# Folding the softmax normalisation into the attention loop and coarsening the interleaved weight quantisation, on eight cores

## The chip, the cores and the metric

The kernel runs on the 8 cores of one Trainium2 chip, each core with half of one sequence of four. The metric is the device time in microseconds of the slowest core. There is no traffic between the cores; each works out keys and values for its whole sequence of 4096 tokens and everything else for its own 2048 tokens.

## The reference

The reference is one transformer layer: multi-head attention with low-rank projections and a rotary part, then a feed-forward block whose weights are quantised to three levels and whose activations are quantised to 8 bits.

```python
attn = softmax(einsum('bhqd,bhkd->bhqk', query, key) / scale)     # 16 heads of 64
out = einsum('bhqk,bhkd->bhqd', attn, value)
x = x + layernorm(out @ Wo + bo)
m = mean(abs(w)); wq = clip(round(w / m), -1, 1) * m              # w_gate, w_up, w_down
x = x + layernorm(bitlinear(silu(bitlinear(h, gate)) * bitlinear(h, up), down))
```

The division by the sum of the softmax can be made after the product with the values. That division, and the quantisation of the three weights, are what the change is about.

## The kernel before

Every operation is put into a list for its engine, and a helper writes out each list in order; an engine takes its instructions strictly in that order and waits on semaphores. All compute carries line 335 in the profile and all transfers line 56, since helpers record them, so groups are told apart by tiles: `poolF` is the f32 buffer on chip, `poolB` the bf16 one, `p` are the PSUM banks and `pb` the PSUM bank for bf16 transposes.

The stages follow one another: projections (to line 768), attention, a normalisation pass (lines 1075 to 1107), the output projection with layer norm, and the feed-forward block.

**Attention** (`emit_b_pair`, line 914) runs over 8 pairs of heads. A pair loads its queries, keys and values, and these loads wait for the pair's predecessor to have spilled its result. Then it runs over 4 query tiles of 512; below, one such tile of one pair is a *slot*, so there are 32 slots, numbered 0 to 31. In a slot 32 chunks of 128 keys are worked through: `emit_scores` (three bf16 matmuls per head), the exponential on ScalarE, and `emit_av` (one f32 matmul per head, with a column of ones in the values, so that row 64 of the result is the sum of the exponentials). The scores of a chunk stand ahead of the product of the chunk before it. After the last chunk comes `drive()`, one step of the weight quantisation, and then for each head three VectorE instructions that empty the PSUM bank: the upper bf16 half, the remainder, and the row of sums, which a transfer takes to the buffer `dall`. The first `emit_av` of the next slot waits for these, its scores do not. At the end of the pair two transfers on POOL's queue spill the unnormalised result.

**Weight quantisation** (`make_wquant`, line 809) is cut into 39 steps, of which 32 are driven by the slots and the last 7 follow after the attention. Each of the weights has mean steps (loads and absolute sums on VectorE), a chain (the mean by way of two tiny matmuls, with bank `p[6]`), and quantisation steps: for each tile a load, three VectorE instructions, then for every 8 blocks of 128 columns 8 transposes on TensorE into `pb`, one VectorE copy, and 8 transfers on POOL's queue. The next 8 transposes wait for the 8 transfers to have landed. A tile of `wg` and `wu` has 8 such blocks (one round), a tile of `wd` has 32 (four rounds). The slots go: 0 to 3 means of `wg`, 4 its chain, 5 to 12 its quantisation at 4 tiles a slot, 13 to 16 means of `wu`, 17 chain, 18 to 25 quantisation, 26 to 29 means of `wd`, 30 chain, 31 the first tile of `wd`. Seven tiles of `wd` follow behind the last pair.

**The normalisation pass** waits for the weight `wo`, takes the reciprocal of all sums at once (16 partitions by 2048), and then for each pair loads the two halves from memory, and for each of four query tiles broadcasts the reciprocals over the partitions with a matmul into `p[6]`, adds the halves, multiplies, splits again, and at the end spills. The next pair's loads wait for that spill.

Of the kernel before, what the change touches and what calls it, by code (L numbers as in the profile page):

```python
# [9 lines left out]
ALU = mybir.AluOpType  # L10
# [9 lines left out]
T_OWN = 2048  # L20
NH = 16
# [165 lines left out]
def build_nc():  # L187
# [47 lines left out]
    attnU_hi_s = scr("attnU_hi", (D, T_OWN), BF16)  # L235
    attnU_lo_s = scr("attnU_lo", (D, T_OWN), BF16)
# [31 lines left out]
    sg_all = af.alloc(16)  # L268
    su_all = af.alloc(16)
    sd_all = af.alloc(16)  # L270
    dall = af.alloc(2048)
    PERSIST_F = af.mark()

    identb = ab.alloc(128)
# [2 lines left out]
    P = Prog(nc)  # L277
# [19 lines left out]
    for j, (src_off, dst) in enumerate(((0, bvb_bc), (1024, bwo_bc))):  # L297
        for half in range(2):
# [3 lines left out]
                start=True, stop=True))(),  # L302
                after=[ev_b1, ev_b2, ev_c[6]] + bc_ev[-1:])
# [14 lines left out]
                   after=[ev_s1])  # L318
# [3 lines left out]
        after=[ev_s2, ev_s3])  # L322
# [466 lines left out]
    ab.reset(PERSIST_B)  # L789
    v_sb = af.alloc(4160)  # L790
    aT = [af.alloc(512), af.alloc(512), af.alloc(512), af.alloc(512)]
    dstage = af.alloc(1024)

    qh_sb = ab.alloc(2048); ql_sb = ab.alloc(2048)
    kh_sb = ab.alloc(4096); kl_sb = ab.alloc(4096)
# [1 line left out]

    wtile0 = af.alloc(4096)
    qa = af.alloc(4096)
    qb = af.alloc(4096)  # L800
    wtile = [wtile0, qa]
    rcols = af.alloc(32)
    wt_b = ab.alloc(4096)
# [1 line left out]

    wq_steps = []
    wq_last = [e_mcols]

    def make_wquant(wdram, ntiles, ncols, nblk, wT_scr, m_col, thr_col):
        st_ = {"prev": [None], "prev_l": [None, None], "prev_tr": [None],  # L810
# [18 lines left out]
        def chain():  # L829
            def go():  # L830
                red_evs = st_["red"]
                e_acc = E("vector", red_evs, "reduce_sum", cols[:, 28:29],
                          rcols[:, 0:ntiles], axis=AX.X)
                e_ps = E("tensor", [e_acc], "matmul", p[6][0:1, 0:1],
                         cols[:, 28:29], onecol_c[:, 0:1], start=True, stop=True)
# [9 lines left out]
                e_thr = E("scalar", [e_bc], "activation", out=thr_col[:, 0:1],  # L845
                          in_=p[6][:, 4:5], func=ACT.Copy, scale=0.5)
                st_["prev_l"] = [list(wq_last) + [e_m, e_thr]]
                st_["prev_tr"] = [list(wq_last) + [e_m, e_thr]]
                wq_last[:] = wq_last[:] + [e_thr]
            return go  # L850
# [46 lines left out]
    wg_m, wg_c, wg_q, wg_st = make_wquant(wg, 32, D, 8, wgT_s, mgate_c, cols[:, 32:33])  # L897
    wu_m, wu_c, wu_q, wu_st = make_wquant(wu, 32, D, 8, wuT_s, mup_c, cols[:, 33:34])
    wd_m, wd_c, wd_q, wd_st = make_wquant(wd, 8, INNER, 32, wdT_s, mdown_c, cols[:, 34:35])
    wq_steps = (  # L900
        [wg_m(8 * i, 8 * i + 8, [e_mcols]) for i in range(4)] + [wg_c()] +
        [wg_q(4 * i, 4 * i + 4) for i in range(8)] +
        [wu_m(8 * i, 8 * i + 8, [e_mcols]) for i in range(4)] + [wu_c()] +
        [wu_q(4 * i, 4 * i + 4) for i in range(8)] +
        [wd_m(2 * i, 2 * i + 2, [e_mcols]) for i in range(4)] + [wd_c()] +
        [wd_q(i, i + 1) for i in range(8)]
    )

    b_prev_loads = [e_mcols]
    b_prev_spills = list(a2b_done[-1:])  # L910
    attn_spills = []
    wq_slices = []

    def emit_b_pair(pr, start_evs, drive=None):
        loads = []
# [18 lines left out]
        em2 = E("vector", [loads[-1]], "memset", vv[:, :, 129:130], 1.0)  # L934
        ev_ld = loads + [em1, em2]

        dstage_free = {0: list(start_evs), 1: list(start_evs)}
        d_dmas = []
        exp_done = {}
        av_done = {}  # L940
        evac_done = [None, None]
        for qt in range(4):
            def emit_scores(chn):
                par = chn % 2
# [40 lines left out]
                    av_done[(hd_, par)] = e_av  # L985

            emit_scores(0)
            emit_scores(1)
            for chn in range(2, 32):
                emit_av(chn - 2)  # L990
                emit_scores(chn)
            emit_av(30)
            emit_av(31)
            if drive is not None:
                drive()
            for hd_ in range(2):
                e_u = E("vector", [av_done[(hd_, 0)], av_done[(hd_, 1)]],
                        "tensor_copy",
                        au_hi[64 * hd_:64 * hd_ + 64, 512 * qt:512 * qt + 512],
                        p[4 + hd_][0:64, 0:512])  # L1000
                e_u2 = E("vector", [e_u], "tensor_tensor",
                         au_lo[64 * hd_:64 * hd_ + 64, 512 * qt:512 * qt + 512],
                         p[4 + hd_][0:64, 0:512],
                         au_hi[64 * hd_:64 * hd_ + 64, 512 * qt:512 * qt + 512],
                         ALU.subtract)
                slot = (2 * qt + hd_) % 2
                e_d = E("vector", [e_u2] + dstage_free[slot], "tensor_copy",
                        dstage[0:1, 512 * slot:512 * slot + 512],
                        p[4 + hd_][64:65, 0:512])
                e_dd = P.dma("gpsimd",  # L1010
                             dall[2 * pr + hd_:2 * pr + hd_ + 1,
                                  512 * qt:512 * qt + 512],
                             dstage[0:1, 512 * slot:512 * slot + 512],
                             after=[e_d], lane=f"b_d{slot}")
                dstage_free[slot] = [e_dd]
                evac_done[hd_] = e_d
                d_dmas.append(e_dd)
        s1 = P.dma("gpsimd", attnU_hi_s[128 * pr:128 * pr + 128, :],
                   au_hi[:, 0:T_OWN], after=[evac_done[0], evac_done[1]],
                   lane="b_au")  # L1020
        s2 = P.dma("gpsimd", attnU_lo_s[128 * pr:128 * pr + 128, :],
                   au_lo[:, 0:T_OWN], after=[evac_done[0], evac_done[1]],
                   lane="b_au")
        return [s1, s2] + d_dmas[-2:] + [evac_done[0], evac_done[1]]

    pair_done = b_prev_loads
    wq_i = [0]
# [5 lines left out]

    for pr in range(8):
        pair_done = emit_b_pair(pr, pair_done, drive=wq_drive)
        attn_spills += pair_done[:4]
    while wq_i[0] < len(wq_steps):
        wq_steps[wq_i[0]]()
        wq_i[0] += 1
# [7 lines left out]
    ab.reset(PERSIST_B)  # L1047
    xqT_sb = ab.alloc(16384)
    PERSIST_B2 = ab.mark()
    dinv = af.alloc(2048)  # L1050
    dexp = af.alloc(512)
    anf = af.alloc(1024)
    projb2 = [af.alloc(1024), af.alloc(1024)]
    xrow2 = [af.alloc(1024), af.alloc(1024)]
    x2row2 = [af.alloc(1024), af.alloc(1024)]
# [16 lines left out]
    ev_wo = prep_w_hilo(wo, (4, 4), 128, wstage3,  # L1072
                        wo_hi[:, 4096:8192], wo_lo[:, 4096:8192], [ev_wo])

    e_dinv = E("vector", attn_spills + [ev_wo], "reciprocal",
               dinv[0:NH, 0:T_OWN], dall[0:NH, 0:T_OWN])

    cn_done = []
    prev_cn = [e_dinv]
    prev_p6 = [e_dinv]  # L1080
    for pr in range(8):
        lh = P.dma("sync", au_h[:, 0:T_OWN],
                   attnU_hi_s[128 * pr:128 * pr + 128, :], after=prev_cn)
        ll = P.dma("sync", au_l[:, 0:T_OWN],
                   attnU_lo_s[128 * pr:128 * pr + 128, :], after=prev_cn)
        sp_evs = []
        for qt in range(4):
            e_bc2 = E("tensor", [e_dinv] + prev_p6, "matmul", p[6][:, 0:512],
                      sel_sb[0:NH, 128 * pr:128 * pr + 128],
                      dinv[0:NH, 512 * qt:512 * qt + 512], start=True, stop=True)  # L1090
            sl = slice(512 * qt, 512 * qt + 512)
            e_t = E("vector", [e_bc2, lh, ll], "tensor_tensor", anf[:, 0:512],
                    au_h[:, sl], au_l[:, sl], ALU.add)
            e_n = E("vector", [e_t], "tensor_tensor", anf[:, 512:1024],
                    anf[:, 0:512], p[6][:, 0:512], ALU.mult)
            e_h2 = E("vector", [e_n], "tensor_copy", au_h[:, sl],
                     anf[:, 512:1024])
            e_l2 = E("vector", [e_h2], "tensor_tensor", au_l[:, sl],
                     anf[:, 512:1024], au_h[:, sl], ALU.subtract)
            prev_p6 = [e_n]  # L1100
            sp_evs.append(e_l2)
        s1 = P.dma("gpsimd", attnU_hi_s[128 * pr:128 * pr + 128, :],
                   au_h[:, 0:T_OWN], after=sp_evs, lane="cn_sp")
        s2 = P.dma("gpsimd", attnU_lo_s[128 * pr:128 * pr + 128, :],
                   au_l[:, 0:T_OWN], after=sp_evs, lane="cn_sp")
        prev_cn = [s1, s2, sp_evs[-1]]
        cn_done = [s1, s2, sp_evs[-1]]

    def ln_single(src, after, b=36):
        e_s = E("vector", after, "reduce_sum", stats[:, b:b + 1], src, axis=AX.X)  # L1110
# [473 lines left out]
```

How the kernel before makes its waits and increments, by code:

```python
        def run(eng_obj, e):  # L115
# [7 lines left out]
                        if val == 0:  # L123
                            continue
                    elif a.dma and a.lane is None:
                        sem, val = a.sem, max(a.val, q_total_at(a.eng, ev.seq))
                    else:
                        sem, val = a.sem, a.val
                    key = id(sem)
                    if key not in waits or waits[key][1] < val:
                        waits[key] = (sem, val)
                for sem, val in waits.values():
                    eng_obj.wait_ge(sem, val)
                ins = fn(eng_obj)
                if ev.needed and ins is not None:
                    ins.then_inc(ev.sem, 16 if ev.dma else 1)
```

## Time and profile before

| what | us |
|---|---|
| median of 2 runs (10101.92 and 10256.78) | 10179.35 |
| the profiled execution's own time | 9708.83 |
| its span, slowest core (5) | 9707.3 |
| shortest span of a core (0) | 9655.7 |
| PE busy in that span | 6200.5 (64%) |
| DVE busy | 2211.1 (23%) |
| ACT busy | 2218.5 (23%) |
| POOL busy | 885.3 (9%) |

In the profile PE is TensorE's matmuls, PEld its weight loads, DVE VectorE, ACT ScalarE, POOL GpSimd, SP SyncE; PEclk is the granted TensorE clock as a share of full speed. The chain of work that ended last is 58% PE, 15% DVE and 9% DMA. The mean of a busy share says little here, because the stages have different limits: attention is read slot by slot.

### The profile page before, as it was taken

The numbers are of one execution on the slowest core, as the hardware profiler recorded it, in microseconds if no ns is written. First come the engines' busy times: TensorE is split into PE (matmuls) and PEld (weight loads), VectorE is DVE, ScalarE is ACT, GpSimd is POOL, SyncE is SP. The second block draws the span as 40 slices with busy tenths as digits, with TensorE's granted clock in tenths as the row PEclk, the third lists the DMA queues.
The fourth block names the chain that finished last, engine by engine and source line by source line (L and its number), as shares of the span: only waits on it lengthen the run. The fifth ranks groups of instructions, "written<-read, shape, count | busy, mean of one in ns | idle before, by whom it ended". The sixth has DMA issues, their size and how long they took to land.

```text
span 9707.3 us, 78875 instructions; the slowest of 8 cores (9655.7 to 9707.3 us)
## 1 busy us (share of the span) xinstructions
PE 6200.5 (64%) x21142; PEld 1966.1 (20%) x21142; DVE 2211.1 (23%) x2749; ACT 2218.5 (23%) x3070; POOL 885.3 (9%) x1453
## 2 busy tenths in 40 slices
PE   5765556776877667578776766687831255454439
PEld 2332222231211111112111111121210022121214
DVE  3323222221101110111001010111012465534442
ACT  1112111113433223234332322233310011111101
POOL 0100212120000110100001010100023010000000
PEclk8776778888998889799997988899965578677769
DMA  4881222212110010211101001002011223343334
GB/s 88 95 86 52 77 78 74 78 61 70 31 26 18 21 45 14 50 33 31 44 11 46 14 27 39 21 36 61 9 45 55 83 78 117 97 138 113 122 105 139
DMA packets 386848, 588.61 MB, mean 61 GB/s; under 512 B 127195, under 2 KB 287084, under 8 KB 378262
## 3 DMA queue, kind: packets, MB, share of 16 engines
q1 hardware_dynamic: 329366, 436.56, 15.7%
q0 software_dynamic: 57088, 147.00, 7.2%
q8 instruction: 223, 3.65, 0.2%
q14 instruction: 171, 1.40, 0.1%
HBM read 436.52 MB, written 146.80 MB: 60 GB/s over the span
## 4 chain that ended last, share of the span: by engine, by line
PE 58%; DVE 15%; issue 10%; DMA 9%; POOL 4%; ACT 2%; SPq 1%; DVEq 0%; POOLq 0%; ACTq 0%; PEldq 0%
PE p L335 55%; DVE poolF L335 10%; DVE poolB L335 4%; PE pb L335 3%; POOL poolF L335 2%; ACT poolF L335 2%; DMA poolF<-vp 1%; POOL wdT L56 1%; DMA poolF<-lo_sk 1%; SPq L56 1%; POOL wuT L56 1%; POOL wgT L56 1%; DMA wuT<-poolB 1%; DMA wgT<-poolB 1%; DMA poolF<-wd 1%
## 5 line engine op out<-in xcount | busy, mean ns | idle before, releaser
L335 PE MATMUL p<-poolB 128*128 128x512 bf16 (+1 forms) x14976 | 3466.9, 397 | 1052.8 <-DVE poolF L335 783.6
L335 PE MATMUL p<-poolF 128*65 128x512 f32 (+3 forms) x4750 | 2486.7, 611 | 1329.6 <-PE p L335 524.6
L335 ACT ACTIVATE poolF<-p,poolF 128x512 f32<-128x512 f32 x2576 | 1962.3, 762 | 5522.7 <-PE p L335 5354.0
L335 PEld LDWEIGHTS p<-poolB 128*128 128x128 bf16 (+1 forms) x14976 | 1321.9, 99 | 3692.3 <-issue 2759.5
L335 PEld LDWEIGHTS p<-poolF 128*65 128x65 f32 (+3 forms) x4750 | 500.3, 143 | 2735.6 <-issue 2733.2
L335 PE MATMUL pb<-poolB 128*128 128x128 bf16 x1408 | 311.3, 257 | 1095.4 <-DVE poolB L335 460.6
L335 DVE TENSOR_TENSOR poolF<-poolF 128x512 f32<-128x512 f32 (+3 forms) x689 | 452.3, 658 | 1353.0 <-ACT poolF L335 1028.5
L335 DVE COPY poolB<-pb 128x1024 bf16<-128x1024 bf16 (+1 forms) x288 | 128.8, 480 | 2724.1 <-PE pb L335 2722.8
L335 DVE TENSOR_SCALAR poolF<-poolF 128x1024 f32<-128x1024 f32 (+4 forms) x529 | 437.6, 827 | 226.0 <-DMA poolF<-wd 102.4
L335 ACT ACTIVATE poolF<-poolF 128x1024 f32<-128x1024 f32 (+2 forms) x194 | 121.6, 627 | 1404.8 <-DVE poolF L335 1129.9
L335 DVE TENSOR_REDUCE poolF<-poolF 128x1 f32<-128x1024 f32 (+3 forms) x205 | 322.7, 1574 | 349.8 <-ACT poolF L335 168.3
L335 PEld LDWEIGHTS pb<-poolB 128*128 128x128 bf16 x1408 | 142.1, 103 | 1279.1 <-issue 1179.8
L335 DVE CAST poolB<-p 64x512 bf16<-64x512 f32 x64 | 43.7, 683 | 1248.1 <-PE p L335 1240.7
L335 POOL TENSOR_TENSOR poolF<-poolF 128x512 f32<-128x512 f32 (+1 forms) x240 | 252.0, 1050 | 815.6 <-ACT poolF L335 780.4
L56 POOL DMA_DIRECT2D wgT<-poolB x256 | 144.6, 573 | 1205.7 <-DVE poolB L335 1195.3
L56 POOL DMA_DIRECT2D wuT<-poolB x256 | 143.4, 568 | 1209.8 <-DVE poolB L335 1197.7
L56 POOL DMA_DIRECT2D poolF<-poolF x64 | 31.8, 497 | 1615.3 <-DVE poolF L335 1610.7
L56 POOL DMA_DIRECT2D wdT<-poolB x256 | 135.8, 538 | 401.7 <-DVE poolB L335 390.1
L335 DVE CAST poolB<-poolF 128x512 bf16<-128x512 f32 (+1 forms) x102 | 84.6, 830 | 362.6 <-ACT poolF L335 250.0
L335 DVE TENSOR_TENSOR poolB<-poolF,poolB 128x512 bf16<-128x512 f32 (+1 forms) x102 | 152.8, 1498 | 11.3 <-DVE poolB L335 0.9
L335 POOL TENSOR_SCALAR poolF<-poolF 128x1 f32<-128x1 f32 (+1 forms) x196 | 40.4, 206 | 1216.6 <-DVE poolF L335 1200.5
L335 ACT ACTIVATE poolF<-poolB 128x512 f32<-128x512 bf16 x96 | 60.7, 632 | 313.1 <-DVE poolB L335 243.7
(51 smaller groups left out, 821.0 us busy)
## 6 DMA issues: line engine op xcount, KB each, us to landing
poolB<-wgT SPq DMA_DIRECT2D x64, 1024.0 KB, 5.6
poolB<-wuT SPq DMA_DIRECT2D x64, 1024.0 KB, 8.1
poolF<-wg SPq DMA_DIRECT2D x64, 512.0 KB, 3.7
poolF<-wu SPq DMA_DIRECT2D x64, 512.0 KB, 3.7
poolF<-wd SPq DMA_DIRECT2D x16, 2048.0 KB, 8.4
poolF<-x_all SPq DMA_DIRECT2D x8, 2048.0 KB
vp<-poolF POOLq DMA_DIRECT2D x32, 512.0 KB, 34.1
poolF<-vp SPq DMA_DIRECT2D x16, 1024.0 KB
```

What stands on the lines that cost most here:

```text
L56: ev = self.emit(eng, lambda e: e.dma_start(out=out, in_=in_, **kw), after=after, dma=True, lane=lane)
L335: return P.emit(eng, lambda e, _o=op, _a=args, _k=kw: getattr(e, _o)(*_a, **_k), after=after)
```

## The change

1. The normalisation pass and the buffer of sums are taken out. In a slot each head's bank is now emptied by one copy of 65 rows to an f32 buffer (four of them, by head and by parity of the slot), and the transfers of the sums are gone.
2. A new function `flush_norm` normalises one head of one slot: the reciprocal of its row of sums on VectorE (1 partition by 512), a broadcast matmul into `p[6]`, a multiplication, and the split in two halves. It is called behind the copies of the slot when more than two results are pending. So it runs not at all in the first slot of a pair, twice in the second and in the third, and four times in the fourth, of which two behind the loop. The spill of the pair waits for the last of them.
3. The weight quantisation has 20 steps instead of 39: the mean steps are doubled (for `wd` all 8 tiles in one), the quantisation steps have 8 tiles instead of 4 for `wg` and `wu`, and 2 instead of 1 for `wd`. In the new order slots 0 and 1 hold means of `wg`, 2 its chain, 3 to 6 its quantisation, 7 and 8 means of `wu`, 9 chain, 10 to 13 quantisation, 14 means of `wd`, 15 chain, 16 to 19 its quantisation. Nothing is left for behind the attention.
4. The buffer `qb` of the quantisation is bf16 instead of f32, and the users of `p[6]` wait for one another.
5. The loop over the chunks is written in another way; the order of the matmuls that it gives is the same: scores of 0, scores of 1, product of 0, scores of 2, product of 1, to product of 30, product of 31.

```diff
+        def flush_norm(hd_, q0):
+            slot = 2 * hd_ + (q0 % 2)
+            ds = slice(512 * slot, 512 * slot + 512)
+            e_rcp = E("vector", [stage_done[slot]] + dstage_free[slot],
+                      "reciprocal", dstage[0:1, ds], anf_b[slot][64:65, 0:512])
+            e_bcx = E("tensor", [e_rcp] + p6_users, "matmul", p[6][:, 0:512],
+                      onesc_sb[0:1, 0:128], dstage[0:1, ds],
+                      start=True, stop=True)
+            rr = slice(64 * hd_, 64 * hd_ + 64)
+            e_nn = E("vector", [e_bcx] + prod_free[hd_], "tensor_tensor",
+                     prodb[rr, 0:512], anf_b[slot][0:64, 0:512],
+                     p[6][0:64, 0:512], ALU.mult)
...
+            e_hh = E("vector", [e_nn] + au_dep, "tensor_copy",
+                     au_hi[rr, 512 * q0:512 * q0 + 512],
+                     prodb[rr, 0:512])
+            e_ll = E("vector", [e_hh], "tensor_tensor",
+                     au_lo[rr, 512 * q0:512 * q0 + 512],
+                     prodb[rr, 0:512],
+                     au_hi[rr, 512 * q0:512 * q0 + 512],
+                     ALU.subtract)
...
             if drive is not None:
                 drive()
             for hd_ in range(2):
-                e_u = E("vector", [av_done[(hd_, 0)], av_done[(hd_, 1)]],
-                        "tensor_copy",
-                        au_hi[64 * hd_:64 * hd_ + 64, 512 * qt:512 * qt + 512],
-                        p[4 + hd_][0:64, 0:512])
-                e_u2 = E("vector", [e_u], "tensor_tensor",
...
-                e_d = E("vector", [e_u2] + dstage_free[slot], "tensor_copy",
...
-                e_dd = P.dma("gpsimd",
...
+                slot = 2 * hd_ + (qt % 2)
+                e_u = E("vector", [av_done[(hd_, 0)], av_done[(hd_, 1)]]
+                        + slot_free[slot],
+                        "tensor_copy", anf_b[slot][0:65, 0:512],
+                        p[4 + hd_][0:65, 0:512])
+                stage_done[slot] = e_u
+                evac_done[hd_] = e_u
+                pend_n.append((hd_, qt))
+            while len(pend_n) > 2:
+                h0, q0 = pend_n.pop(0)
+                flush_norm(h0, q0)
+        while pend_n:
+            h0, q0 = pend_n.pop(0)
+            flush_norm(h0, q0)
...
-    wq_steps = (
-        [wg_m(8 * i, 8 * i + 8, [e_mcols]) for i in range(4)] + [wg_c()] +
-        [wg_q(4 * i, 4 * i + 4) for i in range(8)] +
...
-        [wd_m(2 * i, 2 * i + 2, [e_mcols]) for i in range(4)] + [wd_c()] +
-        [wd_q(i, i + 1) for i in range(8)]
-    )
+    wq_steps = [
+        wg_m(0, 16, [e_mcols]), wg_m(16, 32, [e_mcols]), wg_c(),
+        wg_q(0, 8), wg_q(8, 16), wg_q(16, 24), wg_q(24, 32),
...
+        wd_m(0, 8, [e_mcols]), wd_c(),
+        wd_q(0, 2), wd_q(2, 4), wd_q(4, 6), wd_q(6, 8),
+    ]
...
-    e_dinv = E("vector", attn_spills + [ev_wo], "reciprocal",
-               dinv[0:NH, 0:T_OWN], dall[0:NH, 0:T_OWN])
...
-    for pr in range(8):
-        lh = P.dma("sync", au_h[:, 0:T_OWN],
-                   attnU_hi_s[128 * pr:128 * pr + 128, :], after=prev_cn)
...
+    cn_done = attn_spills[-2:] + [ev_wo]
```

## Rows read from the trace of the kernel before

**Rows 1.** Engines by stretch; busy (x count) by engine, clock, DMA share, GB/s

```profile
2229.00:7143.00 4914.00, 3612.95 (x10796) 882.22 (x10796) 478.34 (x550) 1600.57 (x2055) 344.68 (x625) 0.90 0.12 32
7143.00:7526.00 383.00, 54.63 (x224) 23.33 (x224) 83.30 (x49) 0.00 (x0) 120.11 (x227) 0.50 0.18 61
...
7556.00:7770.00 214.00, 65.30 (x64) 15.87 (x64) 93.16 (x130) 0.00 (x0) 8.44 (x16) 0.50 0.22 79
```

**Rows 2.** Timeline, VectorE, start of the slots' emptying: start, us, what, [idle before]

```profile
2630.30 0.68 DVE L335 CAST poolB<-p 64x512 bf16<-64x512 f32 x1 [99.33 <-PE p L335]
...
2754.20 0.68 DVE L335 CAST poolB<-p 64x512 bf16<-64x512 f32 x1 [100.34 <-PE p L335]
...
2920.17 0.68 DVE L335 CAST poolB<-p 64x512 bf16<-64x512 f32 x1 [0.17 <-DVE poolF L335]
...
4283.34 0.68 DVE L335 CAST poolB<-p 64x512 bf16<-64x512 f32 x1 [0.17 <-DVE poolB L335]
...
4655.68 0.68 DVE L335 CAST poolB<-p 64x512 bf16<-64x512 f32 x1 [100.03 <-PE p L335]
...
4820.37 0.68 DVE L335 CAST poolB<-p 64x512 bf16<-64x512 f32 x1 [106.55 <-PE p L335]
```

**Rows 3.** Timeline, all engines, the end of the first pair

```profile
2754.35 1.04 PE L335 MATMUL p<-poolF 128*65 128x512 f32 x2 [0.26 <-PE p L335]
...
2760.08 0.56 POOL L56 DMA_DIRECT2D attnU_hi<-poolB  x1
...
2764.70 1.99 SPq L56 DMA_DIRECT2D poolB<-qs_hi  x4
...
2791.26 3.98 PE L335 MATMUL p<-poolB 64*128 64x512 bf16 x12 [35.87 <-DVE poolF L335]
```

**Rows 4.** Timeline, a quantisation step of four tiles behind slot 6

```profile
3221.47 0.69 DVE L335 COPY poolB<-pb 128x1024 bf16<-128x1024 bf16 x1 [6.65 <-PE pb L335]
...
3231.98 0.69 DVE L335 COPY poolB<-pb 128x1024 bf16<-128x1024 bf16 x1 [6.63 <-PE pb L335]
...
3241.15 3.93 PE L335 MATMUL p<-poolB 64*128 64x512 bf16 x12
3241.32 0.69 DVE L335 COPY poolB<-pb 128x1024 bf16<-128x1024 bf16 x1 [5.46 <-PE pb L335]
```

**Rows 5.** Engines by stretch: behind that step, and behind the first mean chain

```profile
3241.00:3249.00 8.00, 7.13 (x17) 1.55 (x17) 4.79 (x7) 3.12 (x4) 5.23 (x10) 0.51 0.12 34
...
2921.00:2934.00 13.00, 11.59 (x25) 2.44 (x24) 6.11 (x8) 4.99 (x8) 1.03 (x2) 0.51 0.29 82
```

**Rows 6.** Timeline, the end of slot 31 and the tiles of wd behind it

```profile
7137.37 0.68 DVE L335 CAST poolB<-p 64x512 bf16<-64x512 f32 x1 [0.17 <-DVE poolB L335]
...
7155.94 2.35 DVE L335 TENSOR_SCALAR poolF<-poolF 128x4096 f32<-128x4096 f32 x1 [0.18 <-DVE poolF L335]
7158.40 4.43 DVE L335 TENSOR_TENSOR poolB<-poolF 128x4096 bf16<-128x4096 f32 x1
...
7165.30 0.69 DVE L335 COPY poolB<-pb 128x1024 bf16<-128x1024 bf16 x1 [2.48 <-PE pb L335]
...
7174.23 0.69 DVE L335 COPY poolB<-pb 128x1024 bf16<-128x1024 bf16 x1 [8.24 <-PE pb L335]
...
7526.42 15.30 SPq L56 DMA_DIRECT2D poolF<-wo  x2
```

**Rows 7.** Timeline, the start of the normalisation pass

```profile
7556.47 12.94 DVE L335 RECIPROCAL poolF<-poolF 16x2048 f32<-16x2048 f32 x1 [0.31 <-DVE poolB L335]
...
7576.45 2.04 PE L335 MATMUL p<-poolF 16*128 16x512 f32 x2 [4.86 <-DVE poolF L335]
...
7578.67 0.69 DVE L335 TENSOR_TENSOR poolF<-poolB 128x512 f32<-128x512 bf16 x1 [1.04 <-PE p L335]
```

**Rows 8.** Groups by form: count, busy, mean ns, idle before

```profile
L335 DVE CAST poolB<-poolF 128x512 bf16<-128x512 f32 x32 | 13.7, 428 | 3.3
...
L335 DVE RECIPROCAL poolF<-poolF 128x1 f32<-128x1 f32 x128 | 20.9, 164 | 72.2 <-ACT poolF L335 47.6 <-POOL poolF L335 15.4 <-DVE poolF L335 8.2
```

More of the change, by code:

```diff
@@ L270, in build_nc @@
     sd_all = af.alloc(16)
-    dall = af.alloc(2048)
     PERSIST_F = af.mark()
@@ L791, in build_nc @@
     aT = [af.alloc(512), af.alloc(512), af.alloc(512), af.alloc(512)]
-    dstage = af.alloc(1024)
+    anf_b = [af.alloc(512) for _ in range(4)]
+    prodb = af.alloc(512)
+    dstage = af.alloc(2048)
     qh_sb = ab.alloc(2048); ql_sb = ab.alloc(2048)
@@ L799, in build_nc @@
     qa = af.alloc(4096)
-    qb = af.alloc(4096)
+    qb = ab.alloc(4096)
     wtile = [wtile0, qa]
@@ L807, in build_nc @@
     wq_last = [e_mcols]
+    p6_users = [e_mcols]
     def make_wquant(wdram, ntiles, ncols, nblk, wT_scr, m_col, thr_col):
@@ L833, in go @@
                           rcols[:, 0:ntiles], axis=AX.X)
-                e_ps = E("tensor", [e_acc], "matmul", p[6][0:1, 0:1],
+                e_ps = E("tensor", [e_acc] + p6_users, "matmul", p[6][0:1, 0:1],
                          cols[:, 28:29], onecol_c[:, 0:1], start=True, stop=True)
@@ L846, in go @@
                           in_=p[6][:, 4:5], func=ACT.Copy, scale=0.5)
+                p6_users[:] = [e_mn, e_m, e_thr]
                 st_["prev_l"] = [list(wq_last) + [e_m, e_thr]]
@@ L899, in build_nc @@
     wd_m, wd_c, wd_q, wd_st = make_wquant(wd, 8, INNER, 32, wdT_s, mdown_c, cols[:, 34:35])
-    wq_steps = (
-        [wg_m(8 * i, 8 * i + 8, [e_mcols]) for i in range(4)] + [wg_c()] +
-        [wg_q(4 * i, 4 * i + 4) for i in range(8)] +
-        [wu_m(8 * i, 8 * i + 8, [e_mcols]) for i in range(4)] + [wu_c()] +
-        [wu_q(4 * i, 4 * i + 4) for i in range(8)] +
-        [wd_m(2 * i, 2 * i + 2, [e_mcols]) for i in range(4)] + [wd_c()] +
-        [wd_q(i, i + 1) for i in range(8)]
-    )
+    wq_steps = [
+        wg_m(0, 16, [e_mcols]), wg_m(16, 32, [e_mcols]), wg_c(),
+        wg_q(0, 8), wg_q(8, 16), wg_q(16, 24), wg_q(24, 32),
+        wu_m(0, 16, [e_mcols]), wu_m(16, 32, [e_mcols]), wu_c(),
+        wu_q(0, 8), wu_q(8, 16), wu_q(16, 24), wu_q(24, 32),
+        wd_m(0, 8, [e_mcols]), wd_c(),
+        wd_q(0, 2), wd_q(2, 4), wd_q(4, 6), wd_q(6, 8),
+    ]
     b_prev_loads = [e_mcols]
@@ L912, in build_nc @@
     wq_slices = []
+    slot_free = {s: [e_mcols] for s in range(4)}
+    dstage_free = {s: [e_mcols] for s in range(4)}
+    prod_free = {0: [e_mcols], 1: [e_mcols]}
     def emit_b_pair(pr, start_evs, drive=None):
@@ L935, in emit_b_pair @@
         ev_ld = loads + [em1, em2]
-        dstage_free = {0: list(start_evs), 1: list(start_evs)}
-        d_dmas = []
         exp_done = {}
@@ L941, in emit_b_pair @@
         evac_done = [None, None]
+        stage_done = {}
+        pend_n = []
+        last_l = {}
+        def flush_norm(hd_, q0):
[10 more added lines that the diff above has]
+                     p[6][0:64, 0:512], ALU.mult)
+            p6_users[:] = [e_nn]
+            au_dep = list(start_evs) if q0 == 0 else []
+            e_hh = E("vector", [e_nn] + au_dep, "tensor_copy",
[6 more added lines that the diff above has]
+                     ALU.subtract)
+            prod_free[hd_] = [e_ll]
+            slot_free[slot] = [e_nn, e_rcp]
+            dstage_free[slot] = [e_bcx]
+            last_l[hd_] = e_ll
         for qt in range(4):
@@ L987, in emit_b_pair @@
             emit_scores(0)
-            emit_scores(1)
-            for chn in range(2, 32):
-                emit_av(chn - 2)
+            for chn in range(1, 32):
                 emit_scores(chn)
-            emit_av(30)
+                emit_av(chn - 1)
             emit_av(31)
@@ L996, in emit_b_pair @@
             for hd_ in range(2):
-                e_u = E("vector", [av_done[(hd_, 0)], av_done[(hd_, 1)]],
-                        "tensor_copy",
-                        au_hi[64 * hd_:64 * hd_ + 64, 512 * qt:512 * qt + 512],
-                        p[4 + hd_][0:64, 0:512])
-                e_u2 = E("vector", [e_u], "tensor_tensor",
[L1002 to L1005, printed above, removed]
@@ L1006, in emit_b_pair @@
-                slot = (2 * qt + hd_) % 2
-                e_d = E("vector", [e_u2] + dstage_free[slot], "tensor_copy",
-                        dstage[0:1, 512 * slot:512 * slot + 512],
-                        p[4 + hd_][64:65, 0:512])
-                e_dd = P.dma("gpsimd",
[L1011 to L1014, printed above, removed]
@@ L1015, in emit_b_pair @@
-                dstage_free[slot] = [e_dd]
-                evac_done[hd_] = e_d
-                d_dmas.append(e_dd)
+                slot = 2 * hd_ + (qt % 2)
[6 more added lines that the diff above has]
+                pend_n.append((hd_, qt))
@@ L1018, in emit_b_pair @@
+            while len(pend_n) > 2:
[4 more added lines that the diff above has]
+            flush_norm(h0, q0)
         s1 = P.dma("gpsimd", attnU_hi_s[128 * pr:128 * pr + 128, :],
-                   au_hi[:, 0:T_OWN], after=[evac_done[0], evac_done[1]],
+                   au_hi[:, 0:T_OWN], after=[last_l[0], last_l[1]],
                    lane="b_au")
         s2 = P.dma("gpsimd", attnU_lo_s[128 * pr:128 * pr + 128, :],
-                   au_lo[:, 0:T_OWN], after=[evac_done[0], evac_done[1]],
+                   au_lo[:, 0:T_OWN], after=[last_l[0], last_l[1]],
@@ L1023, in emit_b_pair @@
                    lane="b_au")
-        return [s1, s2] + d_dmas[-2:] + [evac_done[0], evac_done[1]]
+        return [s1, s2, evac_done[0], evac_done[1]]
     pair_done = b_prev_loads
@@ L1035, in build_nc @@
         pair_done = emit_b_pair(pr, pair_done, drive=wq_drive)
-        attn_spills += pair_done[:4]
+        attn_spills += pair_done[:2]
     while wq_i[0] < len(wq_steps):
@@ L1049, in build_nc @@
     PERSIST_B2 = ab.mark()
-    dinv = af.alloc(2048)
-    dexp = af.alloc(512)
-    anf = af.alloc(1024)
     projb2 = [af.alloc(1024), af.alloc(1024)]
@@ L1073, in build_nc @@
                         wo_hi[:, 4096:8192], wo_lo[:, 4096:8192], [ev_wo])
-    e_dinv = E("vector", attn_spills + [ev_wo], "reciprocal",
-               dinv[0:NH, 0:T_OWN], dall[0:NH, 0:T_OWN])
-    cn_done = []
-    prev_cn = [e_dinv]
-    prev_p6 = [e_dinv]
-    for pr in range(8):
-        lh = P.dma("sync", au_h[:, 0:T_OWN],
-                   attnU_hi_s[128 * pr:128 * pr + 128, :], after=prev_cn)
[L1084 to L1107, printed above, removed]
+    cn_done = attn_spills[-2:] + [ev_wo]
     def ln_single(src, after, b=36):
```

## The prediction, made before the change was run

> **What bounds the kernel now.** I read the engines by stretch first, to find the stages. Attention takes 4914 us, the tiles of `wd` behind it 383 us, and the normalisation pass 214 us [rows 1]. The change touches these three and nothing else, so the sum needs only them. In the pass and behind the attention every engine is mostly idle: they are chains of short operations that wait for one another.
>
> Then I read attention slot by slot, in VectorE's timeline. A plain slot takes 123.9 us, from 2630.30 to 2754.20 [rows 2]. In it TensorE is the bound, at 3.87 us for each of 32 chunks; VectorE has been idle for 99 us before it empties the banks, so work put there costs nothing if TensorE need not wait for it. From slot to slot TensorE loses nothing: the scores of the next slot follow at once. A slot that begins a pair takes 164.7 us, from 4655.68 to 4820.37 [rows 2], so the change of pairs costs 40.8 us: the spill is issued 5.9 us after the first emptying starts, it lands and the loads go out 4.6 us later, and the next matmul follows at 2791.26 [rows 3].
>
> The third view is a quantisation step inside attention. The eight slots 5 to 12 last from 2920.17 to 4283.34 [rows 2], 1363.2 us; without 8 plain slots and 2 changes of pairs 290.4 remain, or 36.3 us a step of 4 tiles. TensorE takes its list in order, so the transposes stand between two slots and nothing of the attention passes them. Only the first tile's load and VectorE work lie under the attention. Each further tile costs a whole round, 10.5 us from copy to copy [rows 4].
>
> **Part by part.** The units are those of the profiled execution, 9708.8 us with what lies around its span.
>
> *The pass goes*: from the reciprocal to the next stage, −214 us [rows 1]. Its loads of `wo` ahead of it stay.
>
> *The tail goes*: from the emptying of slot 31 (7137.37) to the load of `wo` (7526.42) are 389 us [rows 6]. In its place stands the end of the last pair, worked out below: 34 us to the spill, 4.6 to its landing [rows 3], about 0.5 to the load. −350 us.
>
> *The tiles of wd come into the slots*, two a step, 4 steps. The first tile is 4 rounds of 8.93 us (7165.30 to 7174.23) [rows 6], 35.7 us. The second tile's load is long done by then, but its VectorE work stands behind the first tile's last copy: copy 0.69, twice 2.35, 4.43, transposes 2.1, and about 0.8 for the gaps, 12.7 us, then 3 rounds, 39.5 in all. Four steps are 301 us. Three of them are followed by a slot of the same pair, which starts at the low clock (below), 4 us each. Before, one tile stood in slot 31 already, 35.7. Net +277 us. That `qb` is bf16 changes nothing: the subtraction reads one f32 operand as before.
>
> *Doubled steps of wg and wu*: 16 steps of 36.3 become 8 of 36.3 + 4 × 10.5 = 78.3, that is 626.4 against 580.8, +46 us. Per tile, the doubling removes half of the free first tiles. The doubled mean steps cost nothing: they are VectorE and transfers alone, and the 99 us of idle VectorE cover them; if they did not fit, the emptying of the banks would be late and the next slot's first product with it.
>
> *flush_norm* is the dear part. Its reciprocal works on 512 elements of one partition. Nearest row: 2048 elements on 16 partitions took 12.94 us, and one element on 128 partitions 0.164 us [rows 7, 8], so the time goes by the elements in a partition and not by the partitions. I take 12.94 / 4 = 3.24 us. Bounds: below, the 0.68 us of any other instruction of 512 elements [rows 2]; above, the same 3.24, since 12.94 for a quarter of the length is excluded by the 0.164. The Trainium skill, "VectorE: DVE Perf Modes", section "First, the fixed hardware budget", says that a reciprocal iterates with a repeat count of 8; at that page's 0.96 GHz an estimate would be 4.3 us, and the sum would be 66 us higher; the row is a quarter cheaper, and I keep the row.
>
> One call, in VectorE's order: reciprocal 3.24 + 0.1; the broadcast from the end of one VectorE instruction to the start of the next, 2.36 us at the low clock (2.04 of matmul, [rows 7]); multiplication 0.69, cast 0.43, subtraction 0.69 and the gaps between, 2.1. That is 7.8 us. VectorE can't shorten it, because each call's reciprocal stands behind the last call's subtraction.
>
> *In the second and third slot of a pair* two calls stand ahead of the next slot's scores in TensorE's list, and their reciprocals behind both copies of 65 rows. TensorE ends the slot 1.2 us after the first copy starts [rows 3]; the second copy ends at 2.3, the first broadcast at 7.8, the second at 15.5. TensorE stands for 14.3 us where it stood for none. It then starts at the low clock: behind a quantisation step it was granted 0.51 for 8 us [rows 5], which costs 4 us. In six of these sixteen slots (5, 6, 10, 13, 17, 18) a quantisation step stands there anyway, so the clock is low already; there the wait is counted from the last transpose, with its copy, 15.8 us. Three mean chains lower the clock in the kernel before as well [rows 5], and that is now counted once. So 10 × 14.3 + 7 × 4 + 6 × 15.8 = +266 us.
>
> *At the end of a pair* four calls stand ahead of the spill: 2.3 + 4 × 7.8 + 0.5 = 34 us after the first copy starts, against 5.9. The loads of the next pair wait for it, and nothing covers that. 7 changes of pairs × 28 = +196 us. The eighth is in the tail above.
>
> **The sum**: −214 − 350 + 277 + 46 + 266 + 196 = +221 us, 9930 for the profiled execution. The two runs shown lie 4 to 5.7% above it. What changes here is VectorE's, POOL's and the transfers' time, not the volume of matmuls, so I add the same 221 to their median: 10179.35 + 221 = 10400, +2.2%.
>
> The Trainium skill, "TensorE: Matmul & The Clock Gate", section "HAM oscillation — how this bites in real kernels", warns that idle gaps between bursts of matmuls let the clock fall and that each costs its restart; it speaks against this change. By that rule the sum is the one above, without it about 80 us less (first rival). This trace agrees: after the chain, a pause of about a microsecond, it shows 0.51 for 13 us.
>
> **The rivals.**
>
> 1. *The clock stays up* during the two short pauses of a slot. Then a broadcast takes 1 us and there is no restart: 10 × 2 + 7 × 4 = 48 us less in the slots, and 1 us for each of the 32 calls at pair ends, 80 in all. +141, 10320, within 2%. Against it: the half clock behind the chain [rows 5].
>
> 2. *The reciprocal of one partition is cheap*, 0.69 us. All 64 calls lie on the path, 64 × 2.55 = 163 us less: +58, 10237, within 2%. Against it: the 0.164 of 128 partitions. It decides the sign of "slower by over 2%" from a reciprocal of about 3.0 us down.
>
> 3. *The doubled steps hide more than one tile*, if TensorE got to transposes while the attention runs. At most 8 × 42 = 336 us less: −115, 10064, within 2%. Against it: the order of the list.
>
> 4. *Everything in the slots is a little dearer*: a restart like that behind the chain, 13 us at half clock instead of 8 (+18), 0.3 us more of gaps a call (+20), 28 rounds of `wd` half a microsecond longer (+14). +273, 10452, slower.
>
> **How the numbers follow.** Forecast 0.56, rival 1 0.15, rival 2 0.08, rival 3 0.04, rival 4 0.13, and 0.04 for a gain by something that I don't see. 2% are 204 us, about what a measurement of this kernel can tell from no change. The forecast's own range is +141 to +273; 0.45 of its 0.56 lie above 204. Slower: 0.45 + 0.13 = 0.58. Same: 0.11 + 0.15 + 0.08 + 0.04 = 0.38. Faster: 0.04. The range takes these ends and the scatter of the two runs, 78 us to either side of their median, most of it on each side: 10250 to 10525.
>
> **What would show it.** Right: reciprocals of 3.2 us; slots 1, 2 and their like followed by 14 us of idle TensorE and some 8 us at half clock; 28 us more at each change of pairs; steps of 78 us in slots 3 to 6; `wo` loaded 39 us after the last slot; the load of `wo` 5730 us after attention's start, where it was 5297. Wrong: broadcasts of 1 us with the clock up, reciprocals under 1 us, or steps shorter than 70 us. What would break the forecast altogether is a chunk that no longer takes 3.87 us, since the chunks' order in the lists is unchanged.

## The result, and the profile after

The changed kernel is slower by the factor 1.0235, with a 95% interval of 1.0199 to 1.0271: slower is shown, slower by more than 2% is not quite, since the interval starts just under 1.02. Its profiled execution took 9885.9 us, its median over 11 runs is 10142.85 us, and that of the kernel before is now, over 10 runs, 9954.72 us. Of these runs many had a lower TensorE clock on one die or both, whichever kernel it was, and by their times so had both runs of before whose median the forecast took as its base; unless another die or group of cores is named, times, ratios and medians over cores are from here on those of executions without that.

The direction, the ratio (+2.2% forecast, +2.35% measured) and, nearly, the sum by parts came out, the absolute time did not: 10142.85 lies below the stated range of 10250 to 10525, and the 9886 of the profiled execution far below it. Of the changed kernel's four runs behind the ratio one took 9942.3 us and three 9885.3 to 9886.6; by these three against before's 9670.5 to 9676.7 it is 1.022, or +213 us.

The engines by stretch in the changed kernel: attention, the end of the last pair, the load of `wo`, and the rest. The columns are those of [rows 1].

```profile
2175.00:7878.00 5703.00, 3829.06 (x11140) 938.88 (x11140) 781.05 (x710) 1596.25 (x2055) 450.27 (x786) 0.84 0.11 31
7878.00:7917.00 39.00, 9.25 (x11) 2.18 (x10) 21.90 (x18) 0.00 (x0) 1.06 (x2) 0.56 0.07 27
7917.00:7948.00 31.00, 0.00 (x0) 0.00 (x0) 13.44 (x4) 0.00 (x0) 0.00 (x0) 0.50 0.39 136
```

The normalisation pass is gone and the tail of 383 us has become 39, but attention takes 5703 us where it took 4914 [rows 1]. Its mean clock fell from 0.90 to 0.84.

One core's trace could mislead here, since the stage behind the pass takes 1932 to 1977 us on different cores of the kernel before. The medians over the eight cores of both profiled executions are better:

| stretch, median of 8 cores, us | before | after | difference | forecast |
|---|---|---|---|---|
| to the first emptied bank of slot 0 | 2344.2 | 2332.1 | −12 | 0 |
| from there to that of slot 31 | 4740.9 | 5530.6 | +790 | +785 |
| from there to the load of `wo` | 388.0 | 39.1 | −349 | −350 |
| to the first load of the output projection | 245.8 | 31.2 | −215 | −214 |
| from there to the end | 1952.1 | 1935.7 | −16 | 0 |

The forecast column is the sum of the prediction's terms: 277 + 46 + 266 + 196 = 785 for the slots. The three changed stretches give +226 us, against the 221 of the prediction; with the two that were not changed it is +198.

Of the other signs that the prediction named, the load of `wo` comes 5742 us after attention's start (5730 forecast, 5703 + 39 in the stretches above).

**The flush between two slots.** The timeline of the changed kernel behind slot 21, all engines but the weight loads:

```profile
6390.57 1.04 PE L334 MATMUL p<-poolF 128*65 128x512 f32 x2 [0.26 <-PE p L334]
6391.72 0.69 DVE L334 COPY poolF<-p 65x512 f32<-65x512 f32 x1 [0.61 <-PE p L334]
6392.58 3.34 DVE L334 RECIPROCAL poolF<-poolF 1x512 f32<-1x512 f32 x1 [0.17 <-DVE poolF L334]
6396.06 2.04 PE L334 MATMUL p<-poolF 1*128 1x512 f32 x2 [4.45 <-DVE poolF L334]
6398.21 0.68 DVE L334 TENSOR_TENSOR poolF<-poolF,p 64x512 f32<-64x512 f32 x1 [2.29 <-PE p L334]
6399.06 0.42 DVE L334 CAST poolB<-poolF 64x512 bf16<-64x512 f32 x1 [0.17 <-DVE poolF L334]
6399.59 0.68 DVE L334 TENSOR_TENSOR poolB<-poolF,poolB 64x512 bf16<-64x512 f32 x1
6400.44 3.34 DVE L334 RECIPROCAL poolF<-poolF 1x512 f32<-1x512 f32 x1 [0.17 <-DVE poolB L334]
6403.93 2.04 PE L334 MATMUL p<-poolF 1*128 1x512 f32 x2 [5.83 <-DVE poolF L334]
6405.90 3.90 PE L334 MATMUL p<-poolB 64*128 64x512 bf16 x12
```

TensorE's last product ends at 6391.6 and its next scores start at 6405.9: 14.3 us, as worked out. From one reciprocal to the next are 7.86 us (7.8 forecast). The reciprocal took 3.34 us (3.24). Both broadcasts took 2.04 us, the low clock's time, although TensorE was at full speed until it fell idle, 4.45 us before the first of them.

The granted clock in the stretches of that flush, behind it, and in the rest of the slot:

```profile
6393.00:6407.00 14.00, 5.11 (x9) 1.32 (x9) 8.79 (x7) 0.00 (x0) 0.00 (x0) 0.57 0.00 0
6407.00:6415.00 8.00, 7.13 (x16) 1.52 (x16) 1.04 (x2) 3.11 (x4) 0.00 (x0) 0.50 0.00 1
6415.00:6530.00 115.00, 99.01 (x290) 23.22 (x287) 0.00 (x0) 45.14 (x58) 0.00 (x0) 0.97 0.00 0
```

The 8 us at half clock behind the flush, for which a quantisation step stood model [rows 5], are there, and here they last longer: to about 6421, 15 us behind the start of the scores. Behind the next flush, where the scores start at 6550.6, they are 6 us. The same columns, finer, for both:

```profile
6415.00:6421.00 6.00, 5.31 (x10) 0.81 (x7) 0.00 (x0) 1.56 (x2) 0.00 (x0) 0.50 0.00 0
6421.00:6530.00 109.00, 93.70 (x281) 22.40 (x280) 0.00 (x0) 43.58 (x56) 0.00 (x0) 0.99 0.00 1
...
6551.00:6557.00 6.00, 5.30 (x14) 1.01 (x12) 1.58 (x3) 3.11 (x4) 0.00 (x0) 0.50 0.00 0
6557.00:6675.00 118.00, 101.52 (x302) 24.25 (x302) 0.00 (x0) 46.70 (x60) 0.00 (x0) 0.99 0.00 0
```

**Slots.** VectorE's timeline of the changed kernel, the first copy of slots 20 to 24, to be read against [rows 2]:

```profile
6266.46 0.69 DVE L334 COPY poolF<-p 65x512 f32<-65x512 f32 x1 [126.18 <-PE p L334]
6390.42 0.69 DVE L334 COPY poolF<-p 65x512 f32<-65x512 f32 x1 [121.97 <-PE p L334]
6535.19 0.69 DVE L334 COPY poolF<-p 65x512 f32<-65x512 f32 x1 [127.04 <-PE p L334]
6676.50 0.69 DVE L334 COPY poolF<-p 65x512 f32<-65x512 f32 x1 [123.72 <-PE p L334]
6867.30 0.69 DVE L334 COPY poolF<-p 65x512 f32<-65x512 f32 x1 [126.10 <-PE p L334]
```

Slot 21 takes 124.0 us, as before. Slots 22 and 23, which start behind a flush, take 144.8 and 141.3, that is 20.9 and 17.4 more than 123.9; the stall is 14.3 and 14.2, and the rest differs as the 15 and 6 us at half clock do. The six such slots of the last three pairs average 19.1 more, against 18.3 forecast. Slot 24, behind a change of pairs, takes 190.8 us where it took 164.7 [rows 2]: 26 more, 28 forecast.

The end of that pair in the timeline: the fourth broadcast, the spill, and the next pair's loads.

```profile
6705.56 2.04 PE L334 MATMUL p<-poolF 1*128 1x512 f32 x2 [5.76 <-DVE poolF L334]
6710.25 0.53 POOL L56 DMA_DIRECT2D attnU_hi<-poolB  x1 [599.65 <-DVE poolB L334]
6711.04 0.53 POOL L56 DMA_DIRECT2D attnU_lo<-poolB  x1 [0.25 <-issue]
6714.98 1.72 SPq L56 DMA_DIRECT2D poolB<-qs_hi  x4
```

The spill goes out 33.8 us after the slot's first copy at 6676.50 (34 forecast, 5.9 before), and the loads 4.7 us after it.

### The profile page after: what moved, and what is told of

Its sections match the earlier page's. It is cut to its first block, busy times and chain, and to the rows that moved or that the text cites. A ratio compares the mean times of both kernels' runs of the same rounds, so it can differ in the third digit from the quotient of the medians.

```text
span 9884.1 us, 78569 instructions; the slowest of 8 cores (9846.0 to 9884.1 us)
## 1 busy us (share of the span) xinstructions
PE 6246.7 (63%) x21206; PEld 1971.6 (20%) x21206; DVE 2359.3 (24%) x2748; ACT 2213.1 (22%) x3070; POOL 864.3 (9%) x1373
## 4 chain that ended last, share of the span: by engine, by line
PE 58%; DVE 16%; issue 10%; DMA 8%; POOL 4%; ACT 2%; SPq 1%; DVEq 0%; POOLq 0%; another core or an unknown queue 0%; ACTq 0%
PE p L334 55%; DVE poolF L334 12%; DVE poolB L334 4%; PE pb L334 3%; ACT poolF L334 2%; POOL poolF L334 2%; DMA poolF<-vp 1%; DMA poolF<-lo_sk 1%; DMA wuT<-poolB 1%; POOL wgT L56 1%; POOL wuT L56 1%; DMA wgT<-poolB 1%; SPq L56 1%; POOL wdT L56 1%; DVEq L133 0%
## 5 line engine op out<-in xcount | busy, mean ns | idle before, releaser
L334 PE MATMUL p<-poolB 128*128 128x512 bf16 (+1 forms) x14976 | 3421.5, 394 | 1057.1 <-DVE poolF L334 753.5
L334 PE MATMUL p<-poolF 128*65 128x512 f32 (+3 forms) x4814 | 2573.7, 622 | 1505.5 <-DVE poolF L334 667.1
L334 DVE COPY poolF<-p 65x512 f32<-65x512 f32 (+2 forms) x67 | 45.6, 680 | 1937.2 <-PE p L334 1932.1
L334 DVE TENSOR_SCALAR poolF<-poolF 128x1024 f32<-128x1024 f32 (+4 forms) x457 | 370.6, 811 | 96.6 <-DVE poolF L334 20.6
L334 DVE TENSOR_TENSOR poolB<-poolF,poolB 64x512 bf16<-64x512 f32 (+3 forms) x206 | 288.4, 1400 | 22.5 <-DVE poolB L334 1.4
L334 DVE RECIPROCAL poolF<-poolF 128x1 f32<-128x1 f32 (+1 forms) x192 | 234.8, 1223 | 83.0 <-ACT poolF L334 47.6
L334 DVE CAST poolB<-poolF 64x512 bf16<-64x512 f32 (+2 forms) x134 | 98.0, 731 | 332.3 <-ACT poolF L334 215.6
```

## The experiments

The theory was: every term above is serial time, because TensorE's and VectorE's lists are in order; the parts add up. The rivals were that the coarser steps and not the fold make the kernel slow, that the reciprocals are partly hidden, that the clock costs nothing, and that the two parts influence one another.

**The coarser steps alone.** The kernel before with the new list of steps:

```diff
-    wq_steps = (
-        [wg_m(8 * i, 8 * i + 8, [e_mcols]) for i in range(4)] + [wg_c()] +
...
+    wq_steps = [
+        wg_m(0, 16, [e_mcols]), wg_m(16, 32, [e_mcols]), wg_c(),
+        wg_q(0, 8), wg_q(8, 16), wg_q(16, 24), wg_q(24, 32),
...
```

> The kernel before, with the 20 coarser quantisation steps of the changed one and nothing else of it; the normalisation pass stays. Theory (TensorE's list is in order, every tile but a step's first is a whole round): 378 us of tail go, 277 come back with wd in the slots, 46 with the doubled steps of wg and wu, so 55 us faster than before, ratio 0.994. Rival (the coarse steps are what makes the changed kernel slow, the folded normalisation is about free): some 200 us slower, ratio 1.02.

In one of these four runs the last core of die 0 ended at 9616 us, where before's fastest run took 9682. More runs of the same kernel:

> The coarser steps alone once more, since the first time neither die was at its usual clock in most runs. Theory: 9616 us as the undisturbed die showed once, 55 to 64 faster than before, ratio 0.994. Rival: slower than before.

Ratio to before 0.993, interval 0.9867 to 0.9994; the fastest four of its runs lie between 9594 and 9612 us, the fastest three of before between 9663 and 9676. In its profile the first to the last slot take 5058.2 us (median of 8 cores), 317 more than before (forecast 277 + 46 = 323), and from slot 31 to `wo` 11.4 us instead of 388.0. The last bank emptied and the load of `wo` in its timeline, against [rows 6]:

```profile
7396.85 0.68 DVE L335 CAST poolB<-p 64x512 bf16<-64x512 f32 x1 [119.04 <-PE p L335]
...
7408.30 0.38 SPq L56 DMA_DIRECT2D poolF<-wo  x1
```

The rival falls: by themselves the coarser steps are a small gain, about 60 us, and it comes from the tail alone. A doubled step of `wg` or `wu` took 78.8 us (median of 8 cores, mean of the eight slots less a plain slot or a change of pairs), 78.3 forecast, so it hid no second tile.

**The fold alone.** The changed kernel with the old list of 39 steps (the same diff, reversed).

> The changed kernel with the 39 quantisation steps of before: the normalisation folded in, the steps untouched. Theory: -214 for the pass, +196 at the changes of pairs and +28 at the last one, and in the sixteen second and third slots 8 x 14.3 + 6 x 4 + 8 x 15.8 = 264, together 274 us slower than before, ratio 1.028; with the run of the steps alone it sums to the changed kernel's 221. Rival (steps are the cost): within 50 us of before. A second rival (the two interact, since fewer steps fall on flushed slots): the sum of both is off by more than 40 us.

> The folded normalisation with the 39 steps once more, for the same reason. Theory: 9933 us as the undisturbed die showed, 253 to 274 slower than before, ratio 1.027. Rival: under 1.02, so that the two parts would not sum to the changed kernel.

In four runs of the first set the die that finished first ended at 9920 to 9935 us. The fastest run of the second set, a single one, took 9919.5 us, about 250 over before's 9663 to 9676. First to last slot took 5201.3 us (median of cores 0 to 3), 460 more than before (forecast 460). The 28 us that I expected at the last pair's end came as 15: from slot 31 to `wo` 403.5 us against 388.0, since `wo` waits for the tiles of `wd`, and their loads run under the flush. The steps' −66 and the fold's +250 make +184, the changed kernel has +213 by its runs; for the slots 317 + 460 = 777 against 790. The two parts interact by some 10 to 30 us, no more.

**Reciprocals as copies.** The sums are not inverted here, so the result is multiplied by them.

```diff
-                      "reciprocal", dstage[0:1, ds], anf_b[slot][64:65, 0:512])
+                      "tensor_copy", dstage[0:1, ds], anf_b[slot][64:65, 0:512])
```

> The changed kernel with the reciprocal of a row of sums replaced by a copy of it, so that the result is multiplied where it should be divided; nothing else is left out. Theory: all 64 reciprocals lie on the path; 3.34 us become about 0.43, so 64 x 2.9 = 186 us less than the changed kernel, about 9700, ratio to before about 1.003. Rival (part of them lies under the landing of transfers or under TensorE's restart): less than 120 us gained.

9714.9 us (one run) against 9885.9, 171 less. The group of that copy on VectorE, by form:

```profile
L334 DVE COPY poolF<-poolF 1x512 f32<-1x512 f32 x64 | 27.2, 425 | 11.1 <-DVE poolB L334 6.9 <-DVE poolF L334 3.8
```

against the changed kernel's

```profile
L334 DVE RECIPROCAL poolF<-poolF 1x512 f32<-1x512 f32 x64 | 213.8, 3341 | 11.1 <-DVE poolB L334 6.9 <-DVE poolF L334 3.8
```

VectorE worked 186.6 us less. From the first slot to `wo` the median core took 5378.8 us instead of 5569.7, 191 less. So all 64 reciprocals lie on the path. Without them the changed kernel as a whole is 33 us above before's fastest run of the same set, 9681.7. Of the fold's own +250, 60 to 80 us would be left, an estimate from 250 less 191 or 171: the broadcasts and the rest of the chain still stand between the slots.

**The clock kept up.** Matmuls with no use, in place of idle waiting, in pairs 5 to 7:

```diff
+            for k in range(fill):
+                E("tensor", [exp_done[(0, 0)], exp_done[(0, 1)]] if k == 0 else [],
+                  "matmul", p[0][:, 0:512], identb[:, 0:128],
+                  qh_sb[:, 0:512], start=True, stop=True)
...
+                flush_norm(h0, q0, fill=(0 if pr < 5 or qt == 3 else
+                                         (18 if h0 == 0 else 24)))
```

> The changed kernel with 18 and 24 idle-filling bf16 matmuls of 512 columns into a scores bank ahead of the two broadcasts of the second and third slots of pairs 5 to 7, where no quantisation stands; their result is overwritten by the next scores. Theory: the clock stays up, so the distance from the slot's first copy to the next slot's falls from 144.8 and 141.3 us to about 137 in these six slots, some 30 us in all. Rival (the stall is VectorE's chain alone and the clock costs nothing): the distances stay. If the filling is longer than the wait: they grow.

The timeline behind slot 21 of this kernel, the filling and the broadcasts, and then the granted clock in the flush and behind it:

```profile
6391.77 3.83 PE L334 MATMUL p<-poolB 128*128 128x512 bf16 x17
...
6396.17 1.09 PE L334 MATMUL p<-poolF 1*128 1x512 f32 x2 [0.57 <-DVE poolF L334]
6397.19 5.35 PE L334 MATMUL p<-poolB 128*128 128x512 bf16 x24
...
6403.09 1.09 PE L334 MATMUL p<-poolF 1*128 1x512 f32 x2 [0.54 <-DVE poolF L334]
```

```profile
6393.00:6404.00 11.00, 9.89 (x41) 3.83 (x38) 8.15 (x5) 0.00 (x0) 0.00 (x0) 1.00 0.00 0
6404.00:6412.00 8.00, 6.77 (x25) 1.84 (x24) 1.80 (x3) 4.60 (x6) 0.00 (x0) 1.00 0.01 3
```

The broadcasts take 1.09 us instead of 2.04 and the clock stays at 1.00, that is 2.4 GHz. The six slots behind such a flush average 137.8 us instead of 143.0 (core 0), 31 us in all. The first slot to the last is 25 us shorter by the median core (5505.8 against 5530.6). What the fall of the clock costs is thus measured: 5 us for each slot that starts behind a flush of two heads, of which 2 in the two broadcasts and 3 behind; I had put it at 6. It was measured in these six slots only.

**The flush moved.** Now the flush of a slot's two results stands in the middle of the next slot, and the pair's end goes into the next pair:

```diff
             for chn in range(1, 32):
                 emit_scores(chn)
                 emit_av(chn - 1)
+                if chn in (8, 14):
+                    flush_one()
...
-        return [s1, s2, evac_done[0], evac_done[1]]
+        return [evac_done[0], evac_done[1]]
```

The result buffers are doubled, and the spill is issued by the flush that completes a pair.

> The changed kernel with the flush moved: each pending head is flushed behind chunks 8 and 14 of the NEXT slot, so that its reciprocal is done long before its broadcast comes up in TensorE's list; the last two of a pair are flushed in the first slot of the next pair, from a second pair of result buffers, and the next pair's loads wait for the emptied banks only, not for the spill. Theory: the stalls of the slots (266 us), of the pairs' ends (196) and 15 of the last one go, the loads start 8 us earlier at 7 changes of pairs (57), and 64 broadcasts cost TensorE about 1.3 us each (83): 451 us less than the changed kernel, about 9435, ratio to before 0.975. Rival (VectorE or bank 6 becomes late and stalls the chunks): less than 300 us gained.

Ratio to before 0.9795, interval 0.9753 to 0.9837, so faster, if not clearly by 2%; 9478 and 9481 us. TensorE's timeline in slot 23 of this kernel, around one broadcast:

```profile
6301.60 1.04 PE L334 MATMUL p<-poolF 128*65 128x512 f32 x2 [0.25 <-PE p L334]
6302.90 1.09 PE L334 MATMUL p<-poolF 1*128 1x512 f32 x2 [0.26 <-PE p L334]
6303.92 1.34 PE L334 MATMUL p<-poolB 64*128 64x512 bf16 x6
```

The broadcast waits for nothing and costs 1.3 us; a slot takes 126.6 us with two of them. A change of pairs takes 159.4 − 126.6 = 32.8 us, where the changed kernel had 66.9 and the kernel before 40.8: the loads no longer wait for the spill. The same instructions are all there; the 64 reciprocals of 3.34 us are now hidden, and of the flush only the broadcasts show, 2.7 us a slot or some 85 us in all. The gain over the changed kernel is 405 us, against 451 expected. From the first slot to `wo` the median core took 5135.9 us instead of 5569.7, 434 less, so 17 of the missing 46 us lie there; the stages ahead of it and behind it took 15 and 5 us longer by the medians, though nothing in them was changed. Neither is explained by a run.

**Finer steps on top.** Mean steps merged, quantisation steps of 4 tiles and of 1 tile of `wd`, 32 in all:

```diff
+        [wg_m(0, 16, [e_mcols]), wg_m(16, 32, [e_mcols]), wg_c()] +
+        [wg_q(4 * i, 4 * i + 4) for i in range(8)] +
+        [wu_m(0, 32, [e_mcols]), wu_c()] +
+        [wu_q(4 * i, 4 * i + 4) for i in range(8)] +
+        [wd_m(0, 8, [e_mcols]), wd_c()] +
+        [wd_q(i, i + 1) for i in range(8)]
```

> As the late flush, with quantisation steps again of 4 tiles of wg and wu and 1 tile of wd, and the mean steps merged, so that all 32 steps fit the 32 slots. Theory: the doubled steps cost 46 us and the second tiles of wd about 4 each, against 4 us more for each restart: about 50 us less than the late flush with the coarse steps, 9385. Rival (fewer, longer stalls are better for the clock): no gain or a loss.

9393.75 us, a single run, 84 to 87 less than with the coarse steps; the slots account for 65 of it (5047.5, median of cores 0 to 3, against 5112.2), where some 50 were expected. The rest I can't assign. The rival falls: more and shorter stalls are better here than fewer and longer ones, since each step hides one tile.

**Loads ahead of time on top.** Two sets of buffers for queries, keys and values; the next pair's loads go out in a pair's first slot.

```diff
+    v_sb2 = [af.alloc(4160), af.alloc(4160)]
+    qh2 = [ab.alloc(2048), ab.alloc(2048)]; ql2 = [ab.alloc(2048), ab.alloc(2048)]
+    kh2 = [ab.alloc(4096), ab.alloc(4096)]; kl2 = [ab.alloc(4096), ab.alloc(4096)]
...
+                if qt == 0 and chn == 16 and pr < 7:
+                    nxt[0] = emit_loads(pr + 1, pair_free[0])
```

> As the late flush with fine steps, and in addition a second set of buffers for queries, keys and values, filled during the pair before. Theory: at 7 changes of pairs about 33 us of waiting for loads and restart remain in the run without it, and go: 230 us less, about 9155, ratio to before 0.947. Rival (these loads are slowed by, or slow down, the transfers of the quantisation): less than 150 us gained.

> The late flush with fine steps and prefetched loads once more, for an interval, since only one undisturbed run of it was had. Theory: 9185 us, ratio to before 0.949. Rival: the single run was a lucky one, 0.96 or more.

9186.7 us the first time and 9167.2 the second, where the kernel before took 9662 to 9686 in the same sets. Each is a single run, so there is no interval; the quotients are 9186.7 / 9669.8 = 0.950 and 9167.2 / 9664.6 = 0.949. The slots take 4833.9 us, 214 less than the 5047.5 without it (230 expected). A change of pairs with a step of `wd` ahead of it, in this kernel's timeline: the last transposes, the scores of the next pair, and only then the loads, which are those of the pair after.

```profile
5927.81 1.35 PE L334 MATMUL pb<-poolB 128*128 128x128 bf16 x5
5929.23 3.96 PE L334 MATMUL p<-poolB 64*128 64x512 bf16 x12
...
5931.74 1.73 SPq L56 DMA_DIRECT2D poolB<-qs_hi  x4
```

This version beats both kernels, the one before by about 490 us.

## Why the prediction was right in its sum and wrong in its base

**The base** is the step that failed. The prediction noted that the two runs shown lay 4 to 5.7% above the profiled execution (5.6 by its time), and then added its 221 us "to their median", 10179.35. Its reason, that the volume of matmuls does not change, bears on the difference and not on the base: it took for granted that further runs would look like those two. They didn't: before's other eight runs took 9670 to 10138 us, and its median over all ten is 9954.72, 225 under the base. The changed kernel's median is 10142.85. The forecast's range, with 78 us of scatter from two runs, was too narrow for the same reason. The profile had shown its own time at 9708.8 with the cores within 52 us of one another; on that base the forecast was 9930, and the changed kernel's four fastest runs took 9885 to 9942. A range that held both bases would have been the honest one, since nothing read of the trace could say which the next runs would have. What sets the one or the other was not tried. The ratio was hardly touched by that: +2.2% on the one base and +2.3% on the other, 2.35% measured.

**The pass and the tail**, −214 and −350: measured −215 and −349.

**The slots**, +785: measured +790. Within it, the tiles of `wd` and the doubled steps, 323, were 317 in the run of the steps alone; the flush in slots and at pair ends was 460 in the run of the fold alone, as worked out for that run. That the sums fit so well is in part luck, for their terms miss by more, in opposite directions. By the medians of 8 cores, slot by slot, the tiles of `wd` cost 259 us and not 277, the doubled steps 59 and not 46. The changed kernel against the run of the steps alone has 274 us in the slots behind two flushes and not 266, 188 at the seven changes of pairs and not 196, and 8 in slots for which nothing was forecast.

**The reciprocal**, 3.24 us from a quarter of a 16-partition row [rows 7]: measured 3.34, that is 6 us more in 64. It lies above the 3.24 that the prediction also took as its upper bound, and the lower bound, 0.68 for "any other instruction of 512 elements", overlooked the cast of 0.428 us in [rows 8]; the sum hangs on neither. The estimate by the page "VectorE: DVE Perf Modes" of the Trainium skill, section "First, the fixed hardware budget", 4.3 us, is 0.9 too long. Rival 2, a cheap reciprocal on one partition, falls by that row and by the run with copies.

**The clock.** Rival 1 falls. The rule of the Trainium skill, "TensorE: Matmul & The Clock Gate", section "HAM oscillation — how this bites in real kernels", that idle gaps are paid with a restart, holds here: 0.50 behind the flush, 1.00 when the gaps are filled. The row that the prediction called its agreement shows less than that: behind the chain [rows 5] the longest pause was 0.77 us, and why the clock fell there no run shows. The term was mis-sized by about 1 us for each slot behind two flushes: 5 measured, 6 forecast.

**The change of pairs**, +28 each: measured +26. The 40.8 us that it is compared with is of core 5 [rows 2], others have a little more or less.

**Rivals 3 and 4** fall too. The doubled steps hid no second tile (78.8 us each). Of rival 4's dearer details one showed in part, half clock for 15 us behind one flush of two; a call took 7.86 us where 7.8 were forecast, and the tiles of `wd` came cheaper than forecast, not dearer.

What was not in the sum at all: the stages ahead of and behind the changed part were 12 and 16 us shorter by the medians, without any change to them. In the kernel before four of the eight cores took 1968 to 1977 us for the last stage and four 1932 to 1936; in the changed one all took 1933 to 1943. Why they part was not tried.

## What to carry to other kernels

A pass of its own that reloads data looks wasteful, but folding it into the loop paid here only once its chain was taken off the order of the engine that bounds the loop: the same 64 reciprocals and broadcasts cost about 460 us between the slots and some 85 us, the broadcasts alone, in the middle of the next slot, against 214 for the pass. Read where in each in-order list a new instruction stands, and what stands behind it, before reading how busy the engines are. A step that hides only its first piece gets dearer when pieces are merged, and a forecast should be made against the base that the profile shows, with a range that says so where the runs disagree.

## What the runs showed of the hardware that was not expected

A reciprocal on VectorE went by the elements in a partition, 6.3 ns each on 16 partitions (12.94 us for 16 × 2048) and 6.5 on one (3.34 for 1 × 512); 128 × 1 took 0.164; the copy of the same 1 × 512 took 0.425. The first of two broadcasts was already at half clock, after 4.45 us of idle TensorE behind dense work; and the half clock behind one and the same stall of 14.3 us lasted 15 us once and 6 us the next time.
